# Cross-attention and mixture of experts, two layers: the router's product taken from x itself, the last tiles of both attention stages in an order of their own, the combine one step ahead

## The reference

```
x = x + L0_xattn(layernorm(x), ctx)      16 heads of 8, q and k normalised, softmax(q k + bias) v, Wo
x = x + L0_ffn(layernorm(x))             8 experts of 256, top 2
x = x + L1_xattn(layernorm(x), ctx)      16 heads of 64, plus silu(xn Wg) * (xn Wh) Wff2
x = x + L1_ffn(layernorm(x))             8 experts of 512, top 2, scores = xn Wr + br
```

## Time and profile before

| | us |
|---|---|
| median of 3 executions | 516.94 |
| lowest, highest | 515.4, 518.66 |
| the profiled execution | 518.24 |
| its span in the trace | 515.9 |
| PE busy | 480.1 (93%) |
| DVE busy | 367.5 (71%) |
| POOL busy | 305.8 (59%) |
| ACT busy | 239.3 (46%) |

### The profile page before, as it was taken

How to read it: one execution, slowest core, us unless ns; L and a number is a source line. 1 busy time by engine, 2 the same in 40 slices (tenths; PEclk the granted TensorE clock), 3 DMA queues, 4 the chain that set the end, 5 groups by cost and what they waited for, 6 DMA issues and landing times.

```text
span 515.9 us, 11674 instructions
## 1 busy us (share of the span) xinstructions
PE 480.1 (93%) x3505; PEld 413.0 (80%) x3505; DVE 367.5 (71%) x1215; ACT 239.3 (46%) x588; POOL 305.8 (59%) x377
## 2 busy tenths in 40 slices
PE   6777999999998999999869999999999689999997
PEld 5456799899887767776648888888898589999996
DVE  3883799999984433333286999999999646677734
ACT  3454666666653455555623434343424115544321
POOL 6237459888864347777332477776775634576650
PEclk9588999999999999999997999999999979999999
DMA  7999980000000133321352130110000012322007
GB/s 221 368 347 340 367 292 22 21 22 22 22 22 22 31 81 92 92 60 37 122 157 62 52 113 31 32 32 13 21 12 17 21 47 79 84 72 66 32 23 245
DMA packets 43842, 49.16 MB, mean 95 GB/s; under 512 B 7569, under 2 KB 29548, under 8 KB 43783
## 3 DMA queue, kind: packets, MB, share of 16 engines
q1 hardware_dynamic: 38287, 39.57, 24.4%
q0 software_dynamic: 4544, 8.44, 5.0%
q10 hardware_dynamic: 952, 0.43, 0.4%
HBM read 20.97 MB, written 28.35 MB: 96 GB/s over the span
## 4 chain that ended last, share of the span: by engine, by line
PE 78%; DVE 6%; POOL 4%; issue 4%; ACT 3%; SPq 2%; DMA 2%; POOLq 0%; DVEq 0%; ACTq 0%
PE ps L1633 10%; PE ps L1486 7%; PE ps L1622 7%; PE ps L1616 7%; PE ps L1579 5%; PE ps L1557 5%; PE ps L1309 5%; PE ps L1534 3%; PE ps L1398 3%; PE ps L1571 2%; PE ps L1581 2%; PE ps L1608 2%; PE ps L1642 2%; PE ps L1401 2%; PE ps L1466 1%
## 5 line engine op out<-in xcount | busy, mean ns | idle before, releaser
L573 POOL DMA_INDIRECT ys<-ysbs,backs x78 | 76.8, 985 | 50.6 <-issue 22.2
L512 POOL TENSOR_TENSOR qr<-qsm,mhalf 128x16 f32<-128x16 f32 x16 | 47.3, 2956 | 17.7 <-DVE qsm L902 17.6
L1257 DVE TENSOR_TENSOR big<-big,ps 128x256 f32<-128x256 f32 x39 | 16.4, 421 | 44.8 <-ACT big L766 44.8
L505 POOL DMA_INDIRECT rows<-pays,slots x32 | 33.2, 1038 | 20.5 <-DVE slots L1031 11.5
L771 ACT ACTIVATE big<-big 128x512 f32<-128x512 f32 x39 | 24.6, 631 | 38.4 <-PE ps L1633 35.0
L1309 PE MATMUL ps<-ones_f 128*128 128x128 f32 x290 | 40.7, 300 | 1.7 <-POOL empty L415 1.7
L531 POOL TENSOR_TENSOR pp<-pp,rden 128x1232 f32<-128x1232 f32 x16 | 36.1, 2253 | 10.2 <-DVE x L1083 10.1
L543 POOL DMA_INDIRECT rows<-pays,slots x32 | 33.0, 1032 | 14.6 <-DVE slots L1105 8.3
L1622 PE MATMUL ps<-xsT,wups 128*128 128x128 f32 x312 | 41.3, 275 | 0.0
L1633 PE MATMUL ps<-w2b,big 128*128 x312 | 41.2, 275 | 0.0
L1309 PEld LDWEIGHTS ps<-ones_f 128*128 128x128 f32 x290 | 38.8, 215 | 2.3 <-POOL empty L415 1.7
(11 more groups left out here) (285 smaller groups left out, 1274.0 us busy)
## 6 DMA issues: line engine op xcount, KB each, us to landing
rows<-empty SPq DMA_DIRECT2D x68, 258.0 KB, 4.3
xs<-rows SPq DMA_DIRECT2D x78, 64.5 KB, 1.8
region_b<-in_L_ffn_W_dram SPq DMA_DIRECT2D x2, 1024.0 KB, 9.6
yb_all<-ys SPq DMA_DIRECT2D x16, 128.0 KB, 2.1
region_a<-in_L_ffn_W_dram SPq DMA_DIRECT2D x8, 256.0 KB, 2.8
w2b<-in_L_ffn_W_dram SPq DMA_DIRECT2D x8, 256.0 KB, 3.1
keys<-ys SPq DMA_DIRECT2D x8, 256.0 KB, 5.6
ys<-ysbs,backs POOLq DMA_INDIRECT x78
```

The source lines that it names most:

```text
L505: pool.indirect_dma_start(rows[0][:, :], bass.IndirectOffsetOnAxis(slot[t % PB][:, k:k + 1], 0), pay[t % PB][:, k, :], None, bounds_check= ...
L512: pool.tensor_tensor(qr[s], qsm[s], mhalf[:, 0:H], ALU.pow).then_inc(a["qr"], 1)
L573: pool.indirect_dma_start(ys[l][:, :], bass.IndirectOffsetOnAxis(backs[:, j % XB:j % XB + 1], 0), ysb[j % YB], None, bounds_check=2 * T - ...
```

## The change

1. **Router on x.** PE transposes x (waits for `xa`) where it transposed the payload (waited for `xnD`). The router weights are centred once: PE sums their columns, DVE subtracts the mean (`centre`). In layer 0 the scores are then short of the factor r, which `margin` gets at the end by one more operation; in layer 1 `scr` becomes one operation that multiplies by r and adds the bias.
2. **Last tiles of layer 0.** The last two steps are replaced by `drain0` on PE and DVE. The last tiles have PSUM banks of their own for transpose and router product (`routed`), the keep-busy groups go from 18 products to 6 and the one behind the count from 24 to 12.
3. **Last tiles of layer 1.** DVE's last four steps are `drain1`; transpose and router product of the last three tiles come a step earlier on PE; the last `norm` goes from POOL to DVE; POOL writes out payloads ahead of `rsD` in these steps; the last keep-busy group goes from 26 to 24.
4. **Combine a step ahead.** In layer 1 DVE does the combine and the statistics of tile i + 1 in step i, from i = -1 on. `TxA` of tile 1 now waits for `gg` of tile 0 by itself. The keep-busy group ahead of layer 1 goes from 14 to 6, and one of 8 is put ahead of the scores of tile 1.
5. **SP** reads the row numbers of three tiles ahead, the first three before it waits for the indirect DMAs.

```diff
+                first = [first_row(j) for j in range(EARLY)]
...
-                    r = sp.value_load(sched[l][0:1, 1, at(j)], min_val=0, max_val=SLOTS - P)
-                    sp.dma_start(xs[k][:, :], rows[l][bass.ds(r, P), :]).then_inc(xs_in[k], 16)
+                    sp.dma_start(xs[k][:, :], rows[l][bass.ds(first[j], P), :]).then_inc(xs_in[k], 16)
+                    if j + EARLY < NJ:
+                        first.append(first_row(j + EARLY))
...
-                if 0 <= t < NT:
+                if 0 <= t < NT - 1:
                     s = t % 2
 
                     pool.wait_ge(a["rden"], a.count("rden", t + 1))
-                    pool.wait_ge(a["comb"], a.count("comb", min(t + 4, NT)))
+                    pool.wait_ge(a["comb"], a.count("comb", min(t + 5, NT)))
...
-                draining = i >= NT + 2
-                if draining:
-                    root_d(a, i - 6)
...
-                if not draining:
-                    root_d(a, i - 6)
+                root_d(a, i - 6)
...
-                    act.copy(x2T[s], MD[:, P:2 * P]).then_inc(a["x2T"], 1)
+                    act.copy(x2T[s], routed(1, t)[:, P:2 * P]).then_inc(a["x2T"], 1)
...
+            def centre(l):
+
+                dve.wait_ge(pro["wc"], pro.count("wc", l + 1))
+                dve.scalar_tensor_tensor(wr[l][:, :], COL[l], -1.0 / D, wr[l][:, :], ALU.mult, ALU.add).then_inc(pro["wcs"], 1)
...
+            def drain0():
+
+                a, t, last = A[0], NT - 2, NT - 1
+                dve.wait_ge(a["route"], a.count("route", t + 1))
+                choose(a, t, routed(0, t)[:, 2 * P:2 * P + E])
+                dve.wait_ge(a["Wo"], a.count("Wo", NT))
+                dve.wait_ge(a["xb"], a.count("xb", NT))
+                dve.tensor_tensor(x[:, last, :], x[:, last, :], MD[:, 0:D], ALU.add).then_inc(a["xa"], 1)
+                statistics(a, last)
+                place(a, t)
+                dve.wait_ge(a["route"], a.count("route", NT))
+                choose(a, last, routed(0, last)[:, 2 * P:2 * P + E])
+                payload(0, last)
+                place(a, last)
...
+                    dve.wait_ge(a["rden"], a.count("rden", t + 1))
+                    p3 = prob[s][:, 0:HK].rearrange("p (h k) -> p h k", h=H)
+                    dve.tensor_tensor(p3, p3, rden[s].unsqueeze(2).to_broadcast([P, H, KEYS]), ALU.mult).then_inc(a["norm"], 1)
+                    dve.wait_ge(a["ffh"], a.count("ffh", t + 1))
+                    dve.scalar_tensor_tensor(gated[:, t % 4, :], ffbuf[s], 0.5, MA[:, :], ALU.mult, ALU.mult).then_inc(a["fo"], 1)
+                t = i - 6
+                if t < NT:
+                    place(a, t)
+                t = i - 5
+                if t < NT:
+                    s = t % 2
+                    dve.wait_ge(a["route"], a.count("route", t + 1))
+                    dve.wait_ge(a["rsD"], a.count("rsD", t + 1))
+                    dve.scalar_tensor_tensor(scr[s], routed(1, t)[:, 2 * P:2 * P + E], rsD[:, t:t + 1], br_bc[:, :], ALU.mult, ALU.add).then_inc(a["scr"], 1)
+                    dve.wait_ge(a["scr"], a.count("scr", t + 1))
+                    choose(a, t, scr[s])
+                    payload(1, t)
...
+                    dve.tensor_tensor(x[:, t, :], x[:, t, :], MC[:, 0:D], ALU.add).then_inc(a["xa"], 1)
+                    statistics(a, t)
...
-                t = i
+                t = i + 1
...
-                    dve.tensor_tensor(scr[s], MD[:, 2 * P:2 * P + E], br_bc[:, :], ALU.add).then_inc(a["scr"], 1)
+                    dve.scalar_tensor_tensor(scr[s], MD[:, 2 * P:2 * P + E], rsD[:, t:t + 1], br_bc[:, :], ALU.mult, ALU.add).then_inc(a["scr"], 1)
...
+                    for i in range(-1, NT + 2):
+                        step1(i)
+                    for i in range(NT + 2, NT + 6):
+                        drain1(i)
...
-                    pe.wait_ge(a["xnD"], a.count("xnD", t + 1))
-                    tr(MD[:, P:2 * P], pay[t % PB][:, 0, 0:D], ident[:, :]).then_inc(a["Tx2"], 1)
+                    pe.wait_ge(a["xa"], a.count("xa", t + 1))
+                    if t >= 1:
+                        pe.wait_ge(a["rsel"], a.count("rsel", t))
+                    tr(MD[:, P:2 * P], x[:, t, :], ident[:, :]).then_inc(a["Tx2"], 1)
...
+            def drain0():
+
+                a, t, last = A[0], NT - 2, NT - 1
+                transposed(0, t)
+                fold(0, 2)
+                pe.wait_ge(a["on"], a.count("on", NT))
+                tr(MC[:, 2 * P:3 * P], on[last % 2], ident[:, :]).then_inc(a["To"], 1)
+                route(0, t)
+                keep_busy(4, TP[1])
+                rank(a, t)
+                pe.wait_ge(a["oT"], a.count("oT", NT))
+                mm(MD[:, 0:D], oT[last % 2], wo0[:, :], start=True, stop=True).then_inc(a["Wo"], 1)
+                fold(2, 4)
+                transposed(0, last)
+                keep_busy(2, TP[1])
+                route(0, last)
+                fold(4, 6)
+                rank(a, last)
...
-                    keep_busy(14, S[2])
+                    keep_busy(6, S[2])
...
+                    if t == 1:
+                        pe.wait_ge(a["gg"], a.count("gg", 1))
...
+                    if t == 1:
+                        keep_busy(8, TP[1])
...
+                early = i - 7
+                if NT - 3 <= early < NT:
+                    pe.wait_ge(a["sub"], a.count("sub", NT))
+                    transposed(1, early)
...
+                if NT - 3 <= early < NT:
+                    route(1, early)
...
-                keep_busy((24, 26)[l], TP[1])
...
+                keep_busy((12, 24)[l], TP[1])
```

159 lines of the change are left out of this document (112 added, 47 removed).

## The result

The changed kernel takes 514.16 us (median of 20 runs) against 517.69 us for the kernel before (20 runs): ratio 0.9934, interval 0.9917 to 0.9950. That is 3.5 us faster. The forecast was 7.7 us, to 509.2, with 504.5 to 513.5 as its range: the direction was right, the size was not, and the time lies outside the range. The profiled execution took 514.33 us, its span is 512.6. One of the 20 runs of the changed kernel took 2603 us; slow runs like it, here and in the experiments, are left out of every ratio.

What follows compares the result with a forecast made beforehand. PE was taken to bound the kernel, with gains only where the pipeline fills and drains: 3.1 + 2.0 + 2.6 = 7.7 us, from the median of 516.94 to 509.2 us, with a range of 504.5 to 513.5.

Steps and rivals of the forecast that it cites:

- Layer 1, last tiles: 2.6: Last tiles of layer 1 up to the first expert transpose, forecast 2.6 us earlier, from 1.5 to 3.6.
- I take the two as even, and leave x of tile 15 at 408.5: Layer 1's drain: earlier transposes and products of tiles 13 to 15 offset the later `AV` of tile 15; no shift.
- rival D: Layer 1 steady steps: POOL locks out `scr`, 0.97 to 2.20 us a step, total 517.5 to 532.3 us; chance 0.05.
- Start of layer 1: 2.0: Start of layer 1: earlier transposes of tiles 0 to 2 gain 2.0 us, from 1.0 upwards.
- PE is ready at 254.7: gain 1.4: Start of layer 1: 16 fewer counted keep-busy products let PE transpose tile 0 earlier, a gain of 1.4 us.
- rival B: First expert tiles: the clock falls behind the shorter keep-busy group, costing 3.4 us, to 512.6; chance 0.13.
- Rival A: Start of layer 1: the PE clock stays up, saving a further 2.5 us, to 506.7; chance 0.22.
- Layer 0, last tiles: 3.1: Last tiles of layer 0 up to the first expert tile, forecast gain 3.1 us, from 2.0 to 3.9.
- 0.5 of 1.14 for tile 13: Layer 0's drain: of the 1.14 us tile 13's transpose waited for its payload, 0.5 reaches everything behind (0 to 1.1).
- 0.7 given back by DVE: Layer 0's drain: extra DVE work between x and the choice of tile 15 costs 0.7 us (0 to 1.6).
- Steady stretches: 0: Middle of both attention stages: PE has no idle time, so the change gains 0 us there.
- Rival C: One drain gains nothing, as `rsD` of tile 14 waits behind a pair of indirect DMAs; 512.3 us, chance 0.10.

Runs made afterwards that it cites:

- the guard: A wait added to the changed kernel: POOL's norm of tile 14 waits for DVE's payload of tile 12; ratio to the kernel before 0.9892.
- e3_kb16: The changed kernel with 17 and not 24 keep-busy products ahead of the experts of layer 1; 519.95 us, ratio to the kernel before 0.9945.
- e10_kb10_15: The changed kernel with the guard, 10 not 6 keep-busy products ahead of layer 1, 15 not 12 behind layer 0's count; 511.10 us, ratio to before 0.9827.
- e1_guard: The first run of the changed kernel with only the guard added; 516.62 us, ratio to the kernel before 0.9892.

## Why the prediction was wrong

- **"Layer 1, last tiles: 2.6"** is the step that failed. The mechanism came as told (slots at 0.16 us, transposes 0.4 us behind x, pairs apart, keep-busy late), but its premise, "I take the two as even, and leave x of tile 15 at 408.5", did not hold: the payload of tile 12 was locked out for 2.0 us, and the clock fell behind the gap (x of tile 15 25.4 us behind its `TxA`, not 21.8). C went from 36.1 (mean of four) to 37.7 and not to 33.6: 4.1 us of miss, of which the guard gives back 3.4. With the guard it is 22.1, so the two orders were as even as I took them, and the lockout and the clock are the whole of it. I had read the row of such a lockout, 2.36 us for `slots`, priced its removal, and looked for a new one only in `scr` (rival D, which did not come: 225 ns against 167). I did not go through every DVE instruction that stands near the `norm` that remained, and I put at nothing that my own order on POOL let this `norm` begin 0.2 us sooner: before, an indirect DMA had kept it behind the payload.
- **"Start of layer 1: 2.0"** was measured at 0.1 (39.34 to 39.24). The step that failed is "PE is ready at 254.7: gain 1.4". PE was ready as told (14.4 us behind the last expert transpose), but `xnA` was not: I took it from the trace of before, 14.6 us behind that transpose, and it came at 15.5 in the mean. That leaves 0.5 of the 1.4 and opens the gap of 1.05 to 1.77 us (0.2 in one trace, 0.7 in another), and behind one of 1.34 and more the clock fell. The 0.6 for tile 2 came, 0.5, where the clock stayed up. I had this as rival B at the first expert tiles, but not here, where the same was done. Rival A, the clock that stays up further on, was true in two traces (e3_kb16 and e10_kb10_15).
- **"Layer 0, last tiles: 3.1"** was too low: 3.85 to 4.15 us in every trace with part 2, less 0.2 to 0.3 in the six expert tiles behind, and rival B in 3 of 13 traces. The two terms that I took in the middle of their bounds (0.5 of 1.14 for tile 13, 0.7 given back by DVE) were too careful: x of tile 15 comes 18.20 us behind that of tile 12 and not 19.18, so 1.0 arrives where I took 0.5.
- **Steady stretches: 0.** Right in layer 1. In layer 0, x of tile 0 to x of tile 12 went from 82.2 to 81.7, 0.4 us that I had not seen.
- Rival C, one drain that gives nothing since a wait takes the place of the one removed, was nearest in kind and gave 512.3; its mechanism (`rsD` behind a pair of DMAs) did not come in the changed kernel, where everything was late already. With the guard a part of it did: in e1_guard `rsD` of tile 14 starts at 403.11, when the pair ends, and `scr` waits 0.99 us for it. In the sum by traces: 0.4 + 4.05 - 0.3 + 0.1 - 1.6 = 2.6 us, and 3.5 were measured; the rest is within what the clock does to single traces.
- That the pair of profiled executions showed 2.2 us at the start of layer 1, near the forecast 2.0, was luck: 1.1 of it lie between the transposes of tiles 2 and 3, where the one of before had the longest spell at half clock of its four traces (269.2 to 276.0).
